# A two-way Mamba block and two 3x3 convolutions on one core: nine instead of eight states with their input made by TensorE, eleven instead of ten C products on GpSimd, and the orders of the engines written anew

## What is computed

```python
xc, z = split(x @ W_in.T)                     # 256 + 256
xc = silu(causal_conv4(xc) + conv_b)
dbc = xc @ W_x.T                              # 8 for dt, 16 for B, 16 for C
dt = softplus(dbc[..., :8] @ W_dt.T + b_dt)
def step(h, inp):                             # h: (batch, 256, 16)
    dt_t, B_t, C_t, x_t = inp
    dA = exp(dt_t[:, :, None] * A)
    h = dA * h + (dt_t * x_t)[:, :, None] * B_t[:, None, :]
    return h, einsum('bdn,bn->bd', h, C_t)
y = (scan(step) + xc * D_skip) * silu(z)
out = y @ W_out.T
```

## Time and profile before

| what | value |
|---|---|
| median of 3 runs | 858.99 us (858.09 to 859.21) |
| profiled execution, its own time | 859.51 us |
| its span | 857.6 us |
| busy: TensorE (PE) | 760.1 us, 89% |
| VectorE (DVE) | 757.2 us, 88% |
| ScalarE (ACT) | 724.1 us, 84% |
| GpSimd (POOL) | 710.3 us, 83% |
| first scan, last scan start | 42.12 us, 764.95 us |
| the two convolutions | from about 779 us to the end |

### The profile page before, as it was taken

How to read it: one execution, slowest core, us unless ns; L and a number is a source line. 1 busy time by engine, 2 the same in 40 slices (tenths; PEclk the granted TensorE clock), 3 DMA queues, 4 the chain that set the end, 5 groups by cost and what they waited for, 6 DMA issues and landing times.

```text
span 857.6 us, 13007 instructions
## 1 busy us (share of the span) xinstructions
PE 760.1 (89%) x4470; PEld 380.3 (44%) x4470; DVE 757.2 (88%) x482; ACT 724.1 (84%) x1295; POOL 710.3 (83%) x335
## 2 busy tenths in 40 slices
PE   7786989999899999898999998989999986868988
PEld 3533434343445353344353533434534433426866
DVE  2698999999999999999999999999999999984141
ACT  3788999999999999999999999999999999435050
POOL 0477899999999999999999999999999999940000
PEclk9699999999999999999999999999999998898999
DMA  5717143253525151617070717271525244000011
GB/s 141 285 68 249 50 151 148 113 210 105 194 78 216 70 209 48 250 58 265 28 270 26 257 42 248 75 247 50 228 72 195 104 158 165 1 1 1 0 37 62
DMA packets 39146, 110.97 MB, mean 129 GB/s; under 512 B 7244, under 2 KB 9384, under 8 KB 39080
## 3 DMA queue, kind: packets, MB, share of 16 engines
q1 hardware_dynamic: 37724, 109.84, 36.3%
q10 hardware_dynamic: 1356, 0.29, 0.2%
HBM read 106.97 MB, written 3.15 MB: 128 GB/s over the span
## 4 chain that ended last, share of the span: by engine, by line
DVE 33%; issue 20%; ACT 18%; PE 17%; POOL 11%; DMA 0%; ACTq 0%; DVEq 0%; POOLq 0%
DVE state L865 15%; DVE bank L865 12%; PE bank L1225 8%; POOL state L574 5%; ACT bank L654 5%; ACT product L678 5%; POOL state L565 5%; ACT state L665 3%; PE bank L1058 3%; DVE state L875 2%; PE bank L1051 2%; ACT dt L718 1%; ACT L713 1%; PE bank L1037 1%; PE bank L991 1%
## 5 line engine op out<-in xcount | busy, mean ns | idle before, releaser
L574 POOL TENSOR_TENSOR state<-state,wide 128x1024 f32<-128x1024 f32 x159 | 373.0, 2365 | 21.8 <-DVE state L865 21.8
L565 POOL TENSOR_TENSOR state<-u,wide 128x1024 f32<-128x1024 f32 x128 | 301.7, 2369 | 8.2 <-PE bank L1058 8.2
L1058 PE MATMUL bank<-state,ident 64*64 64x512 f32 x2048 | 263.7, 625 | 1.0 <-POOL state L574 0.9
L865 DVE TENSOR_TENSOR_SCAN state<-state,bank 128x1024 f32<-128x1024 f32 x95 | 214.7, 2270 | 1.0 <-PE bank L1051 1.0
L678 ACT ACTIVATE product<-u_tok,b_tok 128x256 f32<-128x256 f32 x512 | 212.4, 496 | 2.3 <-PE bank L1051 1.8
L1051 PE MATMUL bank<-ident,product 128*128 128x128 f32 x1024 | 142.0, 283 | 70.4 <-ACT product L678 26.2
L654 ACT ACTIVATE bank<-dt,a_neg 128x512 f32<-128x512 f32 x256 | 165.5, 677 | 30.4 <-DVE state L865 17.1
L1051 PEld LDWEIGHTS bank<-ident,product 128*128 128x128 f32 x1024 | 114.5, 144 | 166.3 <-issue 91.8
L665 ACT ACTIVATE state<-dt,a_neg 128x512 f32<-128x512 f32 x256 | 166.5, 710 | 0.2 <-PE bank L1058 0.2
L865 DVE TENSOR_TENSOR_SCAN bank<-bank,state 128x1024 f32<-128x1024 f32 x64 | 146.1, 2282 | 1.1 <-ACT bank L654 0.3
L865 DVE TENSOR_TENSOR_SCAN state<-bank,state 128x1024 f32<-128x1024 f32 x64 | 145.2, 2268 | 0.0
(11 more groups left out here) (93 smaller groups left out, 493.9 us busy)
## 6 DMA issues: line engine op xcount, KB each, us to landing
wide<-bc_rows SPq DMA_DIRECT2D x176, 512.0 KB, 6.8
wide<-bc_rows SPq DMA_DIRECT2D x32, 256.0 KB, 3.6
x_t<-in_x_dram SPq DMA_DIRECT2D x4, 512.0 KB, 4.8
out_dram<-x_t SPq DMA_DIRECT2D x8, 256.0 KB, 2.0
k_room<-in_L_conv_w_dram SPq DMA_DIRECT2D x2, 576.0 KB, 13.0
bc_rows<-dbc SPq DMA_DIRECT2D x16, 64.0 KB, 1.6
state<-in_L_conv_W_in_dram SPq DMA_DIRECT2D x2, 256.0 KB, 3.9
x_tok<-in_x_dram ACTq DMA_DIRECT2D x1, 256.0 KB, 3.7
```

Of the source, the lines that this page charges most:

```text
L565: pool.tensor_tensor(tile(n), u[:, :, :], over_halves(b_wide[:, PLAIN.index(s), :]), ALU.mult).then_inc(plain_input, 1)
L574: pool.tensor_tensor(tile(n), tile(n), over_halves(c_wide[:, n % NST, :]), ALU.mult).then_inc(output_pool, 1)
L865: dve.tensor_tensor_scan(flat(target), flat(decay), flat(source), 0.0, ALU.mult, ALU.add).then_inc(scanned, 1)
L1058: return pe.matmul(y_sum[64 * h:64 * h + 64, b, :], weights[rows, :], source[rows, h, :], start=first, stop=last)
```

## The change

The states of three sets are chosen anew, and all tables follow. `TURNED` has nine states instead of eight, so seven are plain; `POOL_C` has eleven instead of ten, so VectorE keeps five C products. `post` moves from between the scan and C product of state 4 to ahead of the scan of state 6. Nothing else in the code changes but the order of some loads on SP; what is computed is the same.

```diff
-TURNED = (1, 3, 6, 7, 10, 13, 14, 15)
+TURNED = (1, 2, 5, 6, 10, 12, 13, 14, 15)
-POOL_C = (0, 1, 2, 3, 7, 8, 10, 12, 14, 15)
+POOL_C = (1, 3, 4, 5, 7, 8, 10, 11, 12, 13, 15)
-B_GROUPS = ((0,), (2,), (4, 5), (8, 9), (11, 12))
+B_GROUPS = ((0,), (3, 4), (7, 8), (9,), (11,))
-PE_TURNS = {1: (3,), 4: (6,), 5: (7,), 8: (10,), 11: (13,), 12: (14,), 13: (15,), 15: (17,)}
+PE_TURNS = {0: (2,), 3: (5,), 4: (6,), 8: (10,), 11: (12, 13), 12: (14,), 14: (15,), 15: (17,)}
...
-DVE_POST = 4
-DVE_OUT = 13
-
-POST_INSIDE = True
+DVE_POST = 6
+DVE_OUT = 14
+
+POST_INSIDE = False
 AT_KERNELS = (8, 9, 10)
 AT_STATS = 8
 AT_EXACT = (11, 12)
-AT_EARLY_OUT = (5, 6, 8, 9)
-AT_EARLY_ADD = (7, 10)
+AT_EARLY_OUT = (7, 8, 10, 11)
+AT_EARLY_ADD = (9, 12)
...
                 spread_b(k, 0)
                 spread_b(k, 1)
+                spread_c(k, 0)
+                spread_c(k, 1)
                 spread_b(k, 2)
-                spread_c(k, 0)
                 spread_b(k, 3)
-                spread_c(k, 1)
                 spread_c(k, 2)
```

36 lines of the change are left out of this document (18 added, 18 removed).

## The result

The changed kernel takes 864.23 us (median of 20 executions, 859.83 to 868.29), the kernel before on the same chip 858.35 us (20 executions, 855.88 to 859.65). The ratio of the two is 1.0073, with an interval of 1.0060 to 1.0087: slower by 0.7%, against a forecast of no change. The profiled execution took 863.86 us, its span is 862.1 us; 4.5 us more than the span before.

The account below looks back on a forecast made before the run. GpSimd was taken to bound the kernel before, ScalarE the changed one. Terms +3.1 (items), -0.9 (item 0), -0.4 (item 1), -1.3 and -0.4 (last item) gave +0.1 on 858.99: 859.1 us, range 856.8 to 864.0.

Parts of the forecast that it names:

- What bounds the kernel now: Repeated items of the kernel before: GpSimd's 44.46 us of work sets the pace, VectorE some 0.3 us behind.
- Part 2: ScalarE, one more set of products (1.60 us): it sets the pace at 44.55 to 44.85 us, +3.1 us in all.
- Part 4: ScalarE's decays into banks: margins of 0.5, 0.4 and none before VectorE's reads; costs nothing while these hold.
- Part 3: TensorE, eight more transposes (1.06 us): not the bound; late turns cost 0.1 to 0.3 us in six items, within Part 2.
- the clock: TensorE's clock dips on most items without a projection; a second dip would make turns up to 1.7 us late.
- Parts 1, 5 and 6: C product moved, GpSimd's 44.46 us unchanged; GpSimd keeps up in the new order; SP's reordered loads cost nothing.
- Part 7: Item 0: -0.9 us (bounds -2 and +1), stall before the kernel copies 2 to 3.5 us; item 1: -0.4 us.
- Part 8: Last item, VectorE sets its length: -1.3 us for the C product, -0.4 us for shorter waits for early outputs.
- The rival "slower": Repeated items: ScalarE's bank decays wait or TensorE is late, 0.2 to 0.5 us each item, 862 to 866 us; chance 0.36.

Follow-up runs that it names:

- e3: The kernel before with GpSimd's C product of state 10 made for half of the tokens only; 859.23 us, ratio 1.0009.
- e8: The kernel before with the C products of state 9 (VectorE) and state 10 (GpSimd) made for half of the tokens only; 858.32 us, ratio 1.0004.
- e13: The changed kernel with VectorE's C product of state 9 made for half of the tokens only; 863.27 us, ratio 1.0062.
- e5: The changed kernel with the turned decays of states 12 and 14 moved earlier in ScalarE's order; 868.94 us, ratio 1.0124.
- e14: The changed kernel with dt by exp and logarithm instead of softplus, and state 6's turned decay moved ahead of state 4's decay; 864.82 us, ratio 1.0074.
- e16: The changed kernel with dt by exp and logarithm from one table set instead of softplus, nothing else; 860.33 us, ratio 1.0028.
- e10: The changed kernel with the convolution's second tap left out on TensorE from item 2 on; 864.48 us, ratio 1.0080.
- e4: The changed kernel with GpSimd's C product of state 10 made for half of the tokens only; 862.93 us, ratio 1.0054.
- e18: The kernel of e14 with ScalarE's products of state 14 issued ahead of the decay of state 11 instead of behind it; 856.41 us, ratio 0.9979.
- e9: The changed kernel with only the turned decay of state 14 moved earlier, between ScalarE's last products and the copy of u; 867.71 us, ratio 1.0118.

## Why the prediction was wrong

The forecast was 859.1 us with a range up to 864.0; it came out at 864.23, slower, just outside. The sum had +0.1 us for the profile, which got +4.5. Of the 4.4 us between them the items give 2.7, item 0 gives 1.8 and the last item with the end 1.1; the earlier first scan, which no term had, takes 1.2 back. Two of the signs named in the prediction came true, ScalarE busy over 44.3 us without a listed wait and VectorE idle by about 1 us before scan 7, and they could not tell ScalarE's own work from the loop. By the steps of the prediction:

- **What bounds the kernel now** was wrong where it says that GpSimd sets today's pace. Its 44.46 us of work are right; e3 and e8 show that taking 1.1 us of it away changes nothing. A sum that meets the mean within 0.02 us was no evidence, the mean being over two kinds of items.
- **Part 2**, ScalarE at 44.55 to 44.85 us, was right about ScalarE's own work: 44.70 us is what e13 shows when the loop is shortened, with 0.19 us in it that ScalarE waits for its own products, and 44.50 is what most items of e5 show without them. But the mean item came out at 44.87 and the gates at 44.90, above the upper bound. Fourteen items at +0.39 instead of +0.22 are 5.4 to 5.6 us instead of the 3.1 (2.7 with item 1).
- **Part 4 is the step that failed.** It saw that the decay of state 11 has no margin against the product of state 9, and priced it at nothing "while these hold". I looked at margins one wait at a time and never added up the path that closes from this wait through scan 7 back to itself. It is 44.90 us long: 0.20 us an item above ScalarE's 44.70, 2.8 us in all, and e14 and e16 show that 1.5 us or more off ScalarE beside it leave it as it is. Whether durations of the trace before would have given the 44.90 is not shown: 0.19 us of it are the wait of a copy of u for the products just ahead of it, and in the order before no such copy stands right behind products. No term of the prediction had that wait either.
- **Part 3 and the clock**: less work on TensorE gains at most 0.1 us an item (e10), and the second dip did not come. Of the 311 windows of 2 us between 94 and 716 us, 14 stand below 0.80 of the clock before, in eight items, and 4 in the changed kernel, in two. It goes down to the lower level (0.50, 1.2 GHz) as in the earlier trace rows, but what TensorE did ahead of a dip differs. In five of the eight items before, the clock falls right behind 3.27 us in which TensorE waited for ScalarE's products (up to 350.40, 394.58, 528.43, 572.67 and 706.37 us; behind a sixth such wait, up to 127.94, no window is under 0.80). In the other three, among them, it had been busy. The changed kernel has no such wait, its longest over the items is 1.36 us; its two dips follow a pair of waits of 0.9 to 1.4 us, and six other items have such a pair and no dip. The Trainium skill (TensorE: Matmul & The Clock Gate, "HAM oscillation — how this bites in real kernels") lays the drop to waits that leave the engine idle. Five dips before agree with that and three do not; the prediction had set one of the three against it. The last dip of the changed kernel, with TensorE busy for 1.29 of the 2 us in which the clock fell:

```profile
396.00:398.00 2.00, 1.29 (x6) 1.32 (x7) 1.97 (x2) 2.00 (x4) 1.94 (x3) 0.68 1.04 419
398.00:400.00 2.00, 2.00 (x11) 1.39 (x14) 2.00 (x2) 1.87 (x5) 2.00 (x2) 0.50 1.04 401
```

- **Parts 1, 5 and 6** held, but for the remark of part 1 that GpSimd is the engine that sets the pace: its busy time is the same, it waits 3.1 us in all for scans, and shortening it changes nothing much (e4).
- **Part 7**, item 0, was forecast at -0.9 and is +0.9 in the profile, beside a first scan 1.2 us earlier. The stall before the kernel copies grew to 3.62 us instead of 2.54, and a second one came behind it; no run takes this apart. VectorE's timeline:

```profile
79.06 0.35 DVE L845 COPY k_t<-bank 128x128 bf16<-128x128 bf16 x2 [3.62 <-PE bank L1012]
...
87.63 2.30 DVE L865 TENSOR_TENSOR_SCAN bank<-state,bank 128x1024 f32<-128x1024 f32 x1 [1.26 <-PE bank L1051]
```

- **Part 8**: -0.6 instead of -1.7. The two waits for outputs went from 1.87 to 0.63 us, better than assumed; the rest of the room was not used.
- **The rival "slower"** (a bank decay of ScalarE that waits, 862 to 866 us) is what happened, at 0.36, and the kind of wait is the one it named. The lower end of its price, 0.2 us in each item, is what was found; the path that makes the wait it did not name.

The terms explain 4.5 us of the profiles; the medians are 5.9 us apart. The changed kernel's executions spread over 8.5 us and those of before over 3.8, and no run here shows why.

## What to carry to other kernels

Engines here were within 2% of each other, and in the changed kernel no engine set the pace by itself. Where that is so, list the waits that have no margin and add up, for each, the path from it through the other engine and back to itself in the next item; the longest such loop is a floor for the item. Here work taken out of that loop by mere order paid (e18), while cheaper work beside it only turned into a wait (e14, e16). And a prediction that finds a wait with no margin should put its price into the sum, not into a condition.

## What the runs showed that I had not expected

- A table load on ScalarE shows as 1.28 us and costs 1.30 from start to start (343.40 to 344.70 in the changed kernel). The Trainium skill (ScalarE: Activation LUTs, "What `ACT_TABLE_LOAD` costs") has the same 1283 ns and some 1.38 us of drain on top, 2.66 us for a switch; the trace disagrees on the drain, no gap stands around the load. Replacing two of them by one pass of two 128 x 512 instructions made ScalarE wait 1.7 (e14) and 1.8 us (e16) before the decay of state 11, where the changed kernel has 0.14: 1.5 to 1.7 us gained.
- A set of products costs 1.60 us, but 1.79 where a copy to the tile that these products read stands behind it. ScalarE then waits for its own last instruction, 0.19 us that no view lists as a wait (352.81 to 354.60 in the changed kernel). With a decay between the two, in e9, the gap is gone. The rows of the changed kernel:

```profile
352.81 1.70 ACT L678 ACTIVATE product<-u_tok,b_tok 128x256 f32<-128x256 f32 x4
354.60 0.60 ACT L621 ACTIVATE u_tok<-bank 128x512 f32<-128x512 f32 x1
```

- Adding 1.60 us of ScalarE work to the kernel before cost 16.9 us, 1.07 in each of the items from 1 to 14 (45.55 against 44.48), where ScalarE had 0.88 us of waits to lose.
